# Experts: the router chain of the next block moved from its first expert step into the last step of the block before

## The chip, the cores and the metric

The kernel runs on one core of one Trainium2 chip. The metric is the device time of one execution in microseconds; before the change the median of 3 runs is 865.36 us (864.72 to 866.4).

The core's engines run their own programs side by side and meet at semaphores: PE (TensorE, matrix products; PEld is its weight load), DVE (VectorE), ACT (ScalarE), POOL (GpSimd) and SP (SyncE, which issues transfers here). Each engine works through its program in the order in which it is written.

## The reference, cut to what matters

Four sublayers, each added to x (4 x 1024 tokens, 256 features), each behind a layer normalization: an attention over 77 context tokens, a mixture of six experts, a second attention over the same context, and a feed-forward layer. The change touches the mixture of experts:

```python
z = jnp.einsum('btd,ed->bte', x, proj_w)
q = jnp.tanh(z / QUANT_TEMP)
dot = jnp.einsum('btd,ed->bte', q, anchors)
logits = -(6.0 - dot) * 0.5 / jnp.clip(routing_temp, 0.1)
topk_logits, topk_idx = jax.lax.top_k(logits, 2)
topk_w = jax.nn.softmax(topk_logits, axis=-1)
...
h = jax.nn.gelu(jnp.einsum('btd,edh->bteh', x, w1))
out = jnp.einsum('bteh,ehd,bte->btd', h, w2, expert_weights)
```

All six experts are computed for all tokens; the router gives each token two weights that aren't zero.

## The kernel before, in words

The 4096 tokens are cut into BLOCKS = 8 blocks of 512 tokens (4 tiles of 128). Each stage (attention 0, experts, attention 1, feed-forward) goes over the 8 blocks, with the work of neighbouring blocks interleaved by hand: each engine has one written-out program, and semaphores tie them together. There is no planner. The expert stage takes the time from about 250 to 443 us.

In the expert stage, g is the block and e, from 0 to 5, the expert's step. The parts, with their lines:

- `hidden(g, e)` (PE, L135): 6 matmuls of 512 columns into one of two HID banks. `gelu` (ACT, L516 and L518) reads the bank twice, into `h` (eh) and its rounded part `hh` (ehh); `rest` (DVE, L587) or `rest_pooled` (POOL, L502, experts 3 and 5) makes `hl` = h - hh (ehl).
- `output(g, e)` (PE, L629): 12 matmuls into the two OUT banks, half of them for each; each half waits until the add of the expert before has emptied its bank. PE runs `output` two steps behind `hidden`: in step e it does hidden(g, e) and then output(g, e-2), in steps 0 and 1 output(g-1, 4) and output(g-1, 5).
- `add(g, e)` (DVE, L597): 4 instructions, x += bank * weight. add(g, 0) needs the weights of the block's router.
- The router chain of a block: `project` (PE, L135 with eph and epl, 6 matmuls onto 6 rows), which waits for both halves of the block's normalized input, xh and xl; `squash` (ACT, L523, tanh); `compare` (PE, L612, 4 small fp32 matmuls into bank RD, which the profile records as 8); `router` (DVE, L555 to L567: logit, 10 comparisons, top, rank, below); `power` (POOL, L508, e to the power of below, 24 elements per partition); and `share` (DVE, L574 to L580, 4 instructions that give the weights).
- The normalization of a later block: `moments` (DVE, L90 to L98) in step 5, `invert` (POOL, L103 rstd and L105 shift), `norm` (ACT, L113, 4 instructions) in step 0 of the next block, `turn` (PE, L121, transposes) in steps 2 and 3, `lead` (ACT, L126) and `norm.rest` (DVE, L130, the low part exl) in steps 3 and 4. So norm.rest of half 1 is written in step 4, behind add(g, 2), and serves the next block.

The programs around the change, each in its order:

- PE, step 5 of block g and steps 0 and 1 of the next (L1507 to L1537): hidden(g, 5), output(g, 3), project(g+1), hidden(g+1, 0), output(g, 4), compare(g+1), hidden(g+1, 1), output(g, 5), hidden(g+1, 2), output(g+1, 0), turn, hidden(g+1, 3), output(g+1, 1), turn, hidden(g+1, 4).
- DVE (L1313 to L1334): rest(4), add(2), norm.rest, add(3), moments, rest(g+1, 0), add(4), router(g+1), rest(g+1, 1), add(5), rest(g+1, 2), share(g+1), add(g+1, 0), add(g+1, 1).
- ACT (L1131 to L1164): gelu(g, 5), squash(g+1), gelu(g+1, 0), norm, gelu(g+1, 1), gelu(g+1, 2), lead. In block 4 a weight copy (L1157) stands behind norm, in blocks 2 and 3 copies of the second attention's keys.
- POOL (L1000 to L1024): power(g), rest_pooled(3), rest_pooled(5), invert for a later block, in some blocks one more split or clear, then power(g+1).

In block 2 PE computes the keys and values of the second attention, which ACT takes from the same bank RD (`kv1_taken`).

Of the kernel before, what the change touches and what calls it, by code (L numbers as in the profile page):

```python
# [19 lines left out]
BLOCKS = B * S // N  # L20
# [786 lines left out]
def build(nc, d, out):  # L807
    m, at0, at1 = memory_map()
    place = Places(nc)
    with ExitStack() as stack:  # L810
# [12 lines left out]
        ex = Experts(nc, sem, place, norm, ps, m)  # L823
# [35 lines left out]
        with nc.Block() as block:  # L859
# [370 lines left out]
            def _(dve):  # L1230
# [82 lines left out]
                for g in range(BLOCKS):  # L1313
                    nm = LN_EXP + g + 1
                    for e in range(E):
                        if e not in ex.POOLED and (g > 0 or e > 1):
                            ex.rest(dve, g, e)
                        if e == 2:
                            ex.share(dve, g)
                        if e >= 2:  # L1320
                            ex.add(dve, g, e - 2)
                        elif g > 0:
                            ex.add(dve, g - 1, e + E - 2)
                        if e == 0 and g > 0:
                            ex.router(dve, g)
                        if e in (3, 4):
                            norm.rest(dve, nm, e - 3, ps[e - 3], ex.xh[(g + 1) % 2] if g + 1 < BLOCKS else att.xh,
                                      ex.xl[(g + 1) % 2] if g + 1 < BLOCKS else att.xl)
                        if e == 5:
                            if g + 2 >= BLOCKS:  # L1330
                                dve.wait_ge(ex.added, 2 * E * (g + 3 - BLOCKS))
                            else:
                                dve.wait_ge(att.added, 2 * (g + 3))
                            norm.moments(dve, nm + 1)  # L1334
# [59 lines left out]
                for k in range(BLOCKS * FC):  # L1394
                    g, c = divmod(k, FC)
# [24 lines left out]
            def _(pe):  # L1420
# [86 lines left out]
                for g in range(BLOCKS):  # L1507
                    nm = LN_EXP + g + 1
                    for e in range(E):
                        if g > 0 or e > 3:  # L1510
                            ex.hidden(pe, g, e)
                        if e >= 2:
                            ex.output(pe, g, e - 2)
                        elif g > 0:
                            ex.output(pe, g - 1, e + E - 2)
                        if e == 0 and g > 0:
                            if g == 3:
                                pe.wait_ge(kv1_taken, 1)
                            ex.compare(pe, g)
                        if e in (2, 3):  # L1520
                            if g == 0:
                                pe.wait_ge(att.added, 2 * (BLOCKS - 1) + e - 1)
                            else:
                                pe.wait_ge(norm.xl_ready, C * (nm - 1) + e - 1)
                            norm.turn(pe, nm, e - 2, ps[e - 2])
                        if g == 2 and e == 1:
                            pe.wait_ge(l1_in, 64)
                            pe.wait_ge(ex.logit_ready, g + 1)
                            for k in range(C):
                                nc.tensor.matmul(ex.RD[:, 64:64 + BT], wk1[:, k, :], ctx[:, k, :], start=(k == 0), stop=(k == C - 1))  # L1530
                            for b in range(B):
                                for k in range(C):
                                    last = nc.tensor.matmul(ex.RD[0:T, 384 + b * DH:384 + (b + 1) * DH], ctx[:, k, b * T:(b + 1) * T],
                                                            wv1[:, k, :], start=(k == 0), stop=(k == C - 1))
                            last.then_inc(k1_done, 1)
                    if g + 1 < BLOCKS:
                        ex.project(pe, g + 1)  # L1537
                pe.wait_ge(wl1_ready, 2)
                for c in range(C):
                    att.queries(pe, l1, BLOCKS, c)  # L1540
# [51 lines left out]
                for k in range(BLOCKS * FC):  # L1592
                    g, c = divmod(k, FC)
# [76 lines left out]
```

## Time and profile before

| what | us |
|---|---|
| median of 3 runs | 865.36 (864.72 to 866.4) |
| the profiled execution, its own time | 866.98 |
| its span in the profile | 865.2 |
| PE busy | 774.8 (90%) |
| DVE busy | 659.9 (76%) |
| ACT busy | 520.1 (60%) |
| POOL busy | 398.4 (46%) |

The profiled execution is one run; the times of rows are from it. Its own time is 1.6 us above the median. Busy shares are means over stages with different limits. A row of a timeline gives the start and length of an instruction or of a merged group, and in brackets the idle time of its engine in front of it with the instruction that ended it. The ends of PE's matmuls are modelled, and consecutive matmuls overlap in the record, so the distance between starts is what they cost.

### The profile page before, as it was taken

The numbers are of one execution on the slowest core, as the hardware profiler recorded it, in microseconds if no ns is written. First come the engines' busy times: TensorE is split into PE (matmuls) and PEld (weight loads), VectorE is DVE, ScalarE is ACT, GpSimd is POOL, SyncE is SP. The second block draws the span as 40 slices with busy tenths as digits, with TensorE's granted clock in tenths as the row PEclk, the third lists the DMA queues.
The fourth block names the chain that finished last, engine by engine and source line by source line (L and its number), as shares of the span: only waits on it lengthen the run. The fifth ranks groups of instructions, "written<-read, shape, count | busy, mean of one in ns | idle before, by whom it ended". The sixth has DMA issues, their size and how long they took to land.

```text
span 865.2 us, 13721 instructions
## 1 busy us (share of the span) xinstructions
PE 774.8 (90%) x4452; PEld 568.9 (66%) x4452; DVE 659.9 (76%) x1576; ACT 520.1 (60%) x942; POOL 398.4 (46%) x323
## 2 busy tenths in 40 slices
PE   4799999999899999999988988988879999899996
PEld 3456556666467787777754544554458888788885
DVE  7657877777768777877777888888777778787784
ACT  3455565555554455544446675666668787788774
POOL 5523322223233433443311221222159998988995
PEclk9999999999999999999988999999999999999999
DMA  6965643355200000001075446555000000000001
GB/s 216 159 164 109 146 78 72 74 107 102 70 0 1 2 3 5 2 1 50 15 97 70 59 60 110 88 75 75 3 1 1 25 1 26 25 25 2 25 25 50
DMA packets 24817, 48.01 MB, mean 55 GB/s; under 512 B 3655, under 2 KB 6856, under 8 KB 24234
## 3 DMA queue, kind: packets, MB, share of 16 engines
q1 hardware_dynamic: 23224, 46.02, 27.8%
q10 hardware_dynamic: 1522, 1.11, 0.4%
q8 instruction: 37, 0.61, 0.3%
q14 instruction: 34, 0.28, 0.1%
HBM read 11.47 MB, written 4.19 MB: 18 GB/s over the span
## 4 chain that ended last, share of the span: by engine, by line
PE 52%; DVE 18%; POOL 11%; issue 7%; ACT 5%; DMA 5%; POOLq 0%; ACTq 0%; DVEq 0%
PE bank L135 15%; PE bank L396 5%; PE bank L371 5%; PE bank L629 5%; PE bank L421 5%; DMA qst<-mt 4%; PE bank L407 4%; DVE mx L327 4%; POOL eex L508 4%; PE bank L777 4%; POOL fy L696 3%; POOL frise L689 3%; PE bank L399 2%; PE bank L121 2%; DVE x L597 2%
## 5 line engine op out<-in xcount | busy, mean ns | idle before, releaser
L301 ACT ACTIVATE pt<-bank 77x512 f32<-77x512 f32 x256 | 146.4, 589 | 123.5 <-PE bank L399 76.4
L327 DVE TENSOR_REDUCE mx<-bank 128x4 f32<-128x308 f32 x256 | 108.9, 471 | 30.3 <-PE bank L374 17.8
L396 PE MATMUL bank<-qst,l_kst 128*77 128x512 f32 (+1 forms) x256 | 106.7, 431 | 19.3 <-DMA qst<-mt 13.3
L696 POOL TENSOR_TENSOR fy<-fpart,fg 128x512 f32<-128x512 f32 x64 | 103.9, 1624 | 9.4 <-DVE fpart L737 4.8
L371 PE MATMUL bank<-l_kblk,qh 128*128 128x308 f32 x256 | 89.7, 366 | 12.0 <-DVE mx L327 9.8
L689 POOL TENSOR_TENSOR frise<-fg,fg 128x512 f32<-128x512 f32 x64 | 90.1, 1408 | 9.0 <-POOL fy L696 4.7
L103 POOL TENSOR_TENSOR rstd<-var,minus_half 128x4 f32<-128x4 f32 x32 | 33.2, 1039 | 127.6 <-DVE var L98 74.9
L396 PEld LDWEIGHTS bank<-qst,l_kst 128*77 128x77 f32 (+1 forms) x256 | 36.8, 148 | 83.2 <-issue 48.8
L277 POOL TENSOR_TENSOR ol<-ot,oh 128x512 fp32r<-128x512 f32 x32 | 43.0, 1345 | 94.2 <-ACT oh L306 62.1
L371 PEld LDWEIGHTS bank<-l_kblk,qh 128*128 128x128 f32 x256 | 49.3, 193 | 55.9 <-issue 46.8
L737 DVE SCALAR_TENSOR_TENSOR fpart<-ffixed,frise 128x512 f32<-128x512 uint16 x64 | 58.6, 915 | 33.0 <-POOL frise L689 32.8
L597 DVE SCALAR_TENSOR_TENSOR x<-bank,eweight,x 128x256 f32<-128x256 f32 x192 | 79.5, 475 | 4.4 <-PE bank L629 4.1
L777 PE MATMUL bank<-fw2h,fyh 128*128 128x256 f32 x256 | 72.3, 282 | 3.5 <-DVE fyl L743 3.5
L407 PE MATMUL bank<-pt,l_vall 128*32 128x512 f32 x512 | 69.4, 614 | 6.4 <-DVE ut L335 3.8
L113 ACT ACTIVATE xn<-x,shift,rstd 128x256 f32<-128x256 f32 x128 | 68.1, 590 | 11.6 <-POOL shift L105 11.6
L777 PE MATMUL bank<-fw2l,fyh 128*128 128x256 f32 x256 | 71.9, 281 | 0.0
L777 PE MATMUL bank<-fw2h,fyl 128*128 128x256 f32 x256 | 71.8, 281 | 0.0
L706 ACT ACTIVATE fg<-ffixed 128x512 f32<-128x512 int16 x64 | 40.4, 632 | 45.4 <-DVE ffixed L731 45.2
L629 PE MATMUL bank<-ew2h,ehh 128*128 128x256 f32 x192 | 56.6, 295 | 10.3 <-DVE x L597 10.3
L629 PE MATMUL bank<-ew2l,ehh 128*128 128x256 f32 x192 | 54.7, 285 | 0.0
L629 PE MATMUL bank<-ew2h,ehl 128*128 128x256 f32 x192 | 54.5, 284 | 0.0
L731 DVE TENSOR_SCALAR ffixed<-bank 128x512 int32<-128x512 f32 x64 | 43.7, 683 | 12.0 <-PE bank L135 11.9
(179 smaller groups left out, 2144.2 us busy)
## 6 DMA issues: line engine op xcount, KB each, us to landing
qst<-qh SPq DMA_DIRECT2D x64, 256.0 KB, 6.7
qst<-ql SPq DMA_DIRECT2D x32, 256.0 KB, 9.0
out<-x SPq DMA_DIRECT2D x8, 512.0 KB, 2.6
qst<-ml SPq DMA_DIRECT2D x8, 480.0 KB
x<-in_x SPq DMA_DIRECT2D x3, 1024.0 KB, 12.7
weights<-in_mlp_w SPq DMA_DIRECT2D x2, 1024.0 KB, 5.1
mraw<-in_mask SPq DMA_DIRECT2D x8, 154.0 KB
x<-in_x SPq DMA_DIRECT2D x2, 512.0 KB, 5.5
```

The costliest lines, as they stand in the source:

```text
L113: last = self.nc.scalar.activation(self.xn[:, t:t + 1, :], self.tile(n, t), ACT.Identity, bias=self.shift[:, t, :], scale=self.rstd[:, t, :])
L135: last = self.nc.tensor.matmul(out, w, a, start=(first and k == 0), stop=(k == len(ops) - 1))
L301: self.nc.scalar.activation(self.pt[0:T, i // 4 % 2, i % 4, :], self.bank_of(G, i)[0:T, :], ACT.Exp).then_inc(self.probs, 1)
L327: self.nc.vector.reduce_max(out, banks[u % len(banks)][:, 0:4 * T].rearrange("q (p par t) -> q p par t", p=2, par=2), AX.X).then_inc(self. ...
L371: last = self.nc.tensor.matmul(bank, self.qh[:, c, tile], keys, start=True, stop=not layer.masked)
L396: last = self.nc.tensor.matmul(out, layer.kst[rows, layer.stack(c * HC + 2 * k + par), b * T:(b + 1) * T], self.qst[rows, self.slot(G), c ...
L407: last = self.nc.tensor.matmul(self.U[32 * k:32 * k + 32, :], layer.vall[:, self.batch(G), layer.value(c * HC + 2 * k + par), :], self.pt[ ...
L597: last = self.nc.vector.scalar_tensor_tensor(tile, part, self.weight[:, g % 2, 2 * k + t, e:e + 1], tile, ALU.mult, ALU.add)
L629: last = self.nc.tensor.matmul(self.OUT[k][:, t * D:(t + 1) * D], a[:, e % self.R, tile], w[:, e, :], start=(j == 0), stop=(j == 2))
L689: self.nc.gpsimd.tensor_tensor(self.rise[:, k % 2, :], self.g1[:, k % self.R, :], self.g0[:, k % self.R, :], ALU.subtract).then_inc(self.r ...
L696: self.nc.gpsimd.tensor_tensor(self.y[:, k % 2, :], self.part[:, k % 2, :], self.g0[:, k % self.R, :], ALU.add).then_inc(self.y_ready, 1)
L777: last = nc.tensor.matmul(self.OUT[2 * (g % 2) + t // 2][:, t % 2 * D:(t % 2 + 1) * D], a[:, k % self.R, t * P:(t + 1) * P], w[:, c, :], s ...
```

## The change: what it does

The next block's projection goes from behind output(g, 3) to in front of it, inside step 5; its comparison goes from step 0 of the next block, behind output(g, 4), to step 5 behind output(g, 3); the router on DVE goes from step 0 of the next block, behind add(g, 4), to step 5 behind add(g, 3) and in front of the moments. The wait for `kv1_taken` goes along with the comparison. The programs of ACT, POOL and SP are unchanged.

```diff
@@ DVE
                         elif g > 0:
                             ex.add(dve, g - 1, e + E - 2)
-                        if e == 0 and g > 0:
-                            ex.router(dve, g)
                         if e in (3, 4):
                             norm.rest(dve, nm, e - 3, ps[e - 3], ex.xh[(g + 1) % 2] if g + 1 < BLOCKS else att.xh,
                                       ex.xl[(g + 1) % 2] if g + 1 < BLOCKS else att.xl)
+                        if e == 5 and g + 1 < BLOCKS:
+                            ex.router(dve, g + 1)
                         if e == 5:
...
@@ PE
                         if g > 0 or e > 3:
                             ex.hidden(pe, g, e)
+                        if e == 5 and g + 1 < BLOCKS:
+                            ex.project(pe, g + 1)
                         if e >= 2:
                             ex.output(pe, g, e - 2)
                         elif g > 0:
                             ex.output(pe, g - 1, e + E - 2)
-                        if e == 0 and g > 0:
-                            if g == 3:
+                        if e == 5 and g + 1 < BLOCKS:
+                            if g == 2:
                                 pe.wait_ge(kv1_taken, 1)
-                            ex.compare(pe, g)
+                            ex.compare(pe, g + 1)
...
-                    if g + 1 < BLOCKS:
-                        ex.project(pe, g + 1)
                 pe.wait_ge(wl1_ready, 2)
```

## Rows read from the trace of the kernel before

**Rows 1.** Busy time by window, from output(g,1) to output(g+1,1); window, its length, engines.

```profile
core 0: us, PE busy (x) PEld busy (x) DVE busy (x) ACT busy (x) POOL busy (x), PEclk, DMA share, GB/s
...
284.47:307.84 23.37, 22.99 (x150) 19.56 (x151) 17.65 (x60) 9.60 (x18) 9.29 (x8) 1.00 0.01 1
...
330.36:352.34 21.98, 21.07 (x130) 17.63 (x131) 17.74 (x60) 11.85 (x23) 7.85 (x5) 1.00 0.00 1
...
374.87:397.38 22.51, 21.01 (x130) 17.61 (x131) 17.74 (x60) 11.33 (x21) 9.90 (x7) 1.00 0.14 48
```

**Rows 2.** The chain of waits, block 6; start, length, what.

```profile
390.76 4.71 POOL eex L508
```

**Rows 3.** Timeline of PE, blocks 6 and 7; start, length, line, tiles, idle before.

```profile
392.38 0.36 PE L629 MATMUL bank<-ew2h,ehh 128*128 128x256 f32 x1
...
395.48 0.40 PE L135 MATMUL bank<-exl,ew1h 128*128 128x512 f32 x1
397.38 0.35 PE L629 MATMUL bank<-ew2h,ehh 128*128 128x256 f32 x1 [1.51 <-DVE x L597]
...
399.25 0.48 PE L135 MATMUL bank<-exh,ew1h 128*128 128x512 f32 x1
...
403.67 0.36 PE L629 MATMUL bank<-ew2h,ehh 128*128 128x256 f32 x1
...
405.17 0.39 PE L135 MATMUL bank<-exh,eph 128*6 128x512 f32 x1
...
406.56 0.39 PE L135 MATMUL bank<-exh,ew1h 128*128 128x512 f32 x1
...
409.46 1.05 PE L612 MATMUL bank<-eanchors,eq 6*128 6x6 f32 x8
```

**Rows 4.** Timeline of ACT, the same stretch.

```profile
406.76 0.59 ACT L523 ACTIVATE eq<-bank 6x512 f32<-6x512 f32 x1 [1.93 <-PE bank L135]
...
410.11 2.08 ACT L113 ACTIVATE xn<-x,shift,rstd 128x256 f32<-128x256 f32 x4 [0.88 <-POOL shift L105]
```

**Rows 5.** Timeline of DVE, the same stretch.

```profile
393.57 0.69 DVE L587 TENSOR_TENSOR ehl<-eh,ehh 128x512 fp32r<-128x512 f32 x1 [0.55 <-ACT ehh L518]
...
398.37 1.66 DVE L597 SCALAR_TENSOR_TENSOR x<-bank,eweight,x 128x256 f32<-128x256 f32 x4 [0.34 <-PE bank L629]
...
402.04 0.69 DVE L587 TENSOR_TENSOR ehl<-eh,ehh 128x512 fp32r<-128x512 f32 x1 [1.42 <-ACT ehh L518]
...
404.22 0.68 DVE L130 TENSOR_TENSOR exl<-bank,exh 128x512 fp32r<-128x512 f32 x1
404.82 1.65 DVE L597 SCALAR_TENSOR_TENSOR x<-bank,eweight,x 128x256 f32<-128x256 f32 x4
406.39 1.39 DVE L90 BATCH_NORM_STATS2 stats<-x 128x6 f32<-128x256 f32 x4
...
411.44 0.23 DVE L555 TENSOR_SCALAR elogit<-bank,ehalf 128x24 f32<-128x24 f32 x1
...
412.96 0.17 DVE L567 TENSOR_TENSOR ebelow<-elogit,etop 128x24 f32<-128x24 f32 x1
...
413.87 1.65 DVE L597 SCALAR_TENSOR_TENSOR x<-bank,eweight,x 128x256 f32<-128x256 f32 x4
```

**Rows 6.** Timeline of POOL, the same stretch.

```profile
408.60 1.01 POOL L103 TENSOR_TENSOR rstd<-var,minus_half 128x4 f32<-128x4 f32 x1 [2.35 <-issue]
...
413.28 4.69 POOL L508 TENSOR_TENSOR eex<-eeuler,ebelow 128x24 f32<-128x24 f32 x1 [3.26 <-DVE ebelow L567]
```

**Rows 7.** Timeline of ACT, block 4, behind norm.

```profile
345.08 0.62 ACT L1157 ACTIVATE l_wqh<-weights 128x512 fp32r<-128x512 f32 x1
```

**Rows 8.** The chain of waits, block 2, keys of the second attention.

```profile
300.63 1.04 PE bank L1530 x4
```

**Rows 9.** Busy time by window, end of the first attention; columns as in rows 1.

```profile
228.00:232.00 4.00, 2.67 (x15) 0.95 (x14) 3.97 (x3) 3.33 (x7) 3.43 (x2) 1.00 0.00 0
232.00:236.00 4.00, 2.65 (x14) 2.60 (x15) 1.47 (x5) 0.00 (x0) 1.20 (x1) 0.79 0.57 163
236.00:240.00 4.00, 4.00 (x24) 2.70 (x23) 1.69 (x3) 0.59 (x1) 0.00 (x0) 0.79 0.04 9
```

## The prediction

> **What bounds the kernel now.** I read the windows first, one for each block of the expert stage, cut where output(g,1) starts. Seven such blocks lie between 262 and 420 us; they take 22.5 us each, with two exceptions [rows 1]: 23.4 us where the keys and values of layer 1 are put in, 22.0 us in the block whose power was shortest. TensorE is busy for 21.0 of 22.5 us at the full granted clock. The chain of waits runs through the power in every block but that of the keys [rows 2]: it takes 4.7 us on GpSimd and is what the change wants to start sooner. In TensorE's timeline [rows 3] the price of that chain shows as one pause per block: the last matmul of hidden(6,3) starts at 395.48 and output(6,1) could follow 0.23 us later, at 395.71, but starts at 397.38. So 1.67 us a block is what a perfect cure of the power chain could give, 12 us over seven blocks.
>
> The next question is which chain comes second. The other engines' timelines [rows 4, 5, 6] show a ring that is nearly as long as the one through the power, and I check it link by link, since the change puts its work into this ring. hidden(6,4) at 399.25 [rows 3] gives rest(4) at 402.04; add(2) and the second exl follow back to back, then add(3) at 404.82 and the moments at 406.39 [rows 5]; rstd at 408.60 [rows 6]; the norm at 410.11, which waited for shift [rows 4]; behind it on the same queue stands the gelu of expert 1, and behind that gelu, on DVE, rest(1) and add(5) at 413.87 [rows 5]. output(7,0) waits for half of add(5): one block earlier (22.51 us) that is 391.36 to 392.38 [rows 3], 1.02 us. From there TensorE needs 397.38 - 392.38 - 1.67 = 3.33 us to output(1) and 399.25 - 397.38 = 1.87 us to hidden(4). The ring is 413.87 + 1.02 + 3.33 + 1.87 - 399.25 = 20.84 us: **the spare of this ring is 22.51 - 20.84 = 1.67 us**, and no more.
>
> **The change, part by part.** No instruction is added or removed. The projection (6 matmuls, 406.56 - 405.17 = 1.39 us [rows 3]), the comparison (4 small matmuls in 8 records, 1.05 us [rows 3]) and the router's 14 DVE instructions (411.44 to 412.96 and 0.20 for the last, 1.72 us [rows 5]) move. The ACT and POOL programs stay. No DMA is issued or moved, and nothing is moved past SP's queue.
>
> 1. *Project before output(3).* Project waits for both halves of exl of the next block. The second is written from 404.22 for 0.68 us [rows 5], so it is there at 404.90; with 0.15 us for the signal (an estimate: 1.02 us less the 0.87 that half an add takes) project starts at 405.05. Today that is hidden, for project starts at 405.17. In its new place TensorE is free for it at about 403.67, where output(3) starts now [rows 3]. **TensorE waits 1.4 us in front of project**, and output(3) is queued behind: it starts at 405.05 + 1.39 = 406.44, 2.77 us later than now.
>
> 2. *add(3)* waits for half of output(3). After a waiting output that was 398.37 - 397.38 = 0.99 us [rows 3, 5], so add(3) starts at 407.43, not 404.82: 2.61 us later (DVE idles meanwhile). It takes 406.39 - 404.82 = 1.57 us, to 409.00.
>
> 3. *Comparison.* Squash starts 0.2 us after project's end now (406.76 [rows 4]), so about 406.65, and takes 0.6 us; output(3) lasts to 407.94, so the comparison does not wait. It ends at 407.94 + 1.05 = 408.99 and the router starts at about 409.05, with nothing lost.
>
> 4. *Router before the moments.* The moments start at 409.05 + 1.72 = 410.77, where they now start at 406.39: **4.4 us late, against a spare of 1.67.** 2.6 us are from project's wait, 1.7 us from the router.
>
> 5. *The rest of the ring.* Moments to rstd 2.21, to the norm 1.51, norm to add(5) 3.76, add(5) to output(0) 1.02 us [rows 3 to 6]: output(7,0) at 419.27 where it now is at 414.89. Then 3.33 + 1.87 us to hidden(7,4) at 424.47. **The block is 25.2 us, 2.7 more than 22.5.**
>
> 6. *The power.* In POOL's program invert stands in front of the next power. Today the power starts 3.26 us after POOL is free [rows 6]; with the change ebelow is there before var, but the power waits behind rstd and shift and starts at about 414.5, later on the clock than the 413.28 of now. It ends at 419.2. DVE is at add(5) until 419.9 and rest(2) until 420.5, so share no longer waits for it; output(7,1) can follow 0.86 (share) + 1.02 us later, at 422.4, and TensorE is there at 419.27 + 3.33 = 422.6. The old pause is gone, as wanted. Two others stand in its place, since DVE reaches add(4) only after router, moments and rest(0), at about 413.4: output(6,5) waits 1.2 us, output(7,0) 1.9 us. The first is covered by the second.
>
> *The blocks that differ.* The block with the 4.17 us power takes 21.98 us now [rows 1]; with the ring as bound that advantage is lost: 0.5 us more. In the same block ACT copies a weight between norm and gelu (0.5 us [rows 7]), now in the ring: 0.5 more. The keys' 2.1 us of matmuls (half of them in [rows 8]) go in front of hidden(2) and are covered by output(0)'s new wait; that block comes out at about 26.0 against 23.37, 0.1 less than the rule. GpSimd's extra splits in two blocks delay the power by 1.3 us, up to where share is anyway. **Sum: 7 x 2.7 + 0.5 + 0.5 - 0.1 = 19.8 us.** The last block has no next router and its tail is unchanged. The profiled execution took 866.98 us (span 865.2) and would become 886.8; the median of the runs is 1.6 us less, 865.36, so I say 885.
>
> *Bounds.* Where I took 0.99 us from output to add, a running output might give 0.9; the signal to project is between 0.05 and 0.3 us; the router's 1.72 may be 1.6. Together 0.3 us a block either way, 2 us in all. The ring's links were seen only with their present neighbours; I allow the same again.
>
> *A rule against the trace.* GpSimd's power is beside DVE work with two SBUF inputs today: rest(2), 393.57, falls into the power of 390.76 to 395.46 and takes 0.69 us, as the one at 402.04 with POOL idle does [rows 2, 5]. The two don't hold each other up here. The Trainium skill ("SBUF — State Buffer", section "SBUF: two separate sides") says the opposite: such a DVE instruction and a GpSimd instruction share a port pair that is locked for the whole instruction, and the other "fully blocks". By it rest(1), ready at 417.6, would wait for the power's end at 419.2, and each block would be 1.6 us longer.
>
> **The rivals.** (A) *Ends faster:* the ring through moments and norm has room that the rows don't show, and only the power chain counts. Place: the norm on ACT. It decides if output(0) would still be there within 22.5 us, so if the moments can be 4.4 us late at no cost. Then the 1.67 us pause goes and the 1.4 us in front of project come, with 0.2 us of small waits gone: -0.5 a block, 862; if in addition project didn't wait, up to 7 x 1.67 = 11.7 us less, 854. Against it: ACT waited for shift in each of the blocks (0.88 us [rows 4]). (B) *Only one delay bites,* the router's 1.7 us or project's 2.6 being hidden: +0.1 to +1.0 us a block, 866 to 872. Against it: both are in front of the moments in one queue. (C) *The clock.* In 228:236 TensorE was busy 5.3 of 8 us, and the granted clock of the 8 us from 232 was 0.79 [rows 9]: of the levels 2.4 and 1.2 GHz the lower one for 8 x 2 x 0.21 = 3.4 us. The new block has 1.2 and 1.9 us of waiting with 2.9 of work between, so 2.9 of 6. If the clock falls there, in TensorE's part of the ring, 3.4 us at half speed cost 1.7 us a block: 897. Against it: after the pause of 1.51 us in front of 397.38 the matmuls keep their pace. (D) *The port lock* above, as a mechanism of this kernel: rest(1) behind the power, +1.6 us a block, 896. Its page is the one named there. (E) *Nothing to see:* the waits only change places.
>
> **How the numbers follow.** Forecast 0.75; A 0.06; B 0.07, of it 0.01 within 0.2%; C 0.09; D 0.02; E 0.01. A measurement of this kernel tells about 0.2%, 1.7 us, from no change. Faster 0.06, same 0.02, slower 0.92. The forecast's own range is 881 to 889. For 8 in 10 I widen it to 875 at the bottom (a part of B) and 893 at the top (a clock that falls in some blocks, C).
>
> **What would show it.** Right: TensorE's idle time in front of project, released by exl, of 1.2 to 1.4 us and seven times; no wait of eexs for the power; the moments some 4.4 us later after output(3)'s old place; waits of output(0) of 1.7 us or more for add(5); ACT's wait for shift in front of the norm longer than 0.88; blocks of 25.2 us. Wrong: blocks of 21 to 22 us, which would mean that the moments had room; project starting straight behind hidden(5), which would break step 1; a power that starts before rstd, which would break step 6; a granted clock under 1.00 in this stage, which would be C.

## The result, and the profile after

| | before | after |
|---|---|---|
| median of 4 runs each, us | 865.04 (864.41 to 866.4) | 889.78 (888.8 to 893.36) |
| ratio | 1 | 1.029 (95%: 1.027 to 1.031) |
| span of the profiled run, us | 865.2 | 887.5 |
| PE busy in it, us | 774.8 | 776.8 |

The change costs 24.7 us; the prediction's sum was 19.8. The measured 889.78 us lies in the wide range of 875 to 893, but above the 881 to 889 that the prediction gave to its forecast itself. In a second measurement it took 888.25 against 865.73 us.

The windows first, as in [rows 1], but cut where the moments of a block start, the event that the prediction turned on. The column PEclk, third from the end, is the granted clock. The two windows that are left out are the block of the keys (301.15 to 326.85, 25.70 us at a clock of 1.00) and the last one.

```profile
core 0: us, PE busy (x) PEld busy (x) DVE busy (x) ACT busy (x) POOL busy (x), PEclk, DMA share, GB/s
274.51:301.15 26.64, 22.58 (x132) 19.00 (x131) 17.65 (x60) 10.13 (x20) 8.26 (x5) 0.94 0.00 1
326.85:351.92 25.07, 21.01 (x133) 17.55 (x132) 17.67 (x61) 13.48 (x28) 9.14 (x6) 1.00 0.02 5
351.92:379.06 27.14, 22.56 (x132) 18.87 (x131) 17.65 (x60) 11.16 (x22) 8.28 (x5) 0.94 0.01 2
379.06:404.14 25.08, 20.99 (x132) 17.54 (x131) 17.66 (x60) 11.13 (x22) 9.56 (x6) 1.00 0.00 1
404.14:430.77 26.63, 22.57 (x133) 19.01 (x131) 17.66 (x61) 10.14 (x20) 9.57 (x6) 0.94 0.12 41
```

Two kinds of block stand there: 25.1 us at a clock of 1.00, and 26.6 us at 0.94 (27.1 in block 4, where the weight copy is). The forecast was 25.2, and 25.7 for block 4. In the long ones TensorE is busy 1.6 us longer with as many instructions. Cut finer, one of them shows where:

```profile
404.14:412.75 8.61, 5.81 (x36) 4.66 (x35) 5.79 (x21) 5.06 (x10) 6.15 (x4) 1.00 0.27 85
412.75:414.00 1.25, 1.25 (x8) 1.25 (x9) 1.25 (x4) 0.00 (x0) 0.83 (x1) 0.78 0.68 275
414.00:417.00 3.00, 3.00 (x14) 2.77 (x13) 2.28 (x8) 0.60 (x1) 0.00 (x0) 0.52 0.00 0
417.00:430.77 13.77, 12.52 (x79) 10.33 (x77) 8.33 (x30) 4.48 (x9) 2.59 (x2) 1.00 0.01 1
```

Behind the wait for output(0), which ends at 412.75, the clock is at its lower level for some 3 us. In windows of 1 us the same shows from 284 to 287, 362 to 366 and 441 to 444: in four of seven blocks.

The timelines of PE, DVE, POOL and ACT around block 7, to be read against [rows 3 to 6]:

```profile
419.45 0.48 PE L135 MATMUL bank<-exh,ew1h 128*128 128x512 f32 x1
425.16 0.40 PE L135 MATMUL bank<-exh,eph 128*6 128x512 f32 x1 [1.25 <-DVE exl L130]
426.55 0.28 PE L629 MATMUL bank<-ew2h,ehh 128*128 128x256 f32 x1
428.06 1.05 PE L612 MATMUL bank<-eanchors,eq 6*128 6x6 f32 x8
434.39 0.36 PE L629 MATMUL bank<-ew2h,ehh 128*128 128x256 f32 x1 [0.87 <-DVE x L597]
439.38 0.36 PE L629 MATMUL bank<-ew2h,ehh 128*128 128x256 f32 x1 [1.94 <-DVE x L597]
```

```profile
424.42 0.68 DVE L130 TENSOR_TENSOR exl<-bank,exh 128x512 fp32r<-128x512 f32 x1
427.45 1.66 DVE L597 SCALAR_TENSOR_TENSOR x<-bank,eweight,x 128x256 f32<-128x256 f32 x4 [2.35 <-PE bank L629]
429.15 0.24 DVE L555 TENSOR_SCALAR elogit<-bank,ehalf 128x24 f32<-128x24 f32 x1
430.77 1.40 DVE L90 BATCH_NORM_STATS2 stats<-x 128x6 f32<-128x256 f32 x4
432.77 0.69 DVE L587 TENSOR_TENSOR ehl<-eh,ehh 128x512 fp32r<-128x512 f32 x1
437.76 0.69 DVE L587 TENSOR_TENSOR ehl<-eh,ehh 128x512 fp32r<-128x512 f32 x1 [2.74 <-ACT ehh L518]
438.37 1.65 DVE L597 SCALAR_TENSOR_TENSOR x<-bank,eweight,x 128x256 f32<-128x256 f32 x4
```

```profile
432.99 1.32 POOL L103 TENSOR_TENSOR rstd<-var,minus_half 128x4 f32<-128x4 f32 x1 [6.54 <-issue]
434.67 4.16 POOL L508 TENSOR_TENSOR eex<-eeuler,ebelow 128x24 f32<-128x24 f32 x1
```

```profile
434.69 2.08 ACT L113 ACTIVATE xn<-x,shift,rstd 128x256 f32<-128x256 f32 x4 [2.87 <-POOL shift L105]
```

Project waits for exl; output(3) stands behind it; add(3) idles DVE for 2.35 us; the router takes its turn, and only then come the moments. GpSimd idled for 6.5 us up to rstd, although the router's result was there 2.1 us earlier, at 430.9: rstd is in front of the power in its program. output(5), at 434.39, and output(0), at 439.38, wait for their adds.

### The profile page after: what moved, and what is told of

It is laid out like the page before. It is cut to its first block, busy times and chain, and to the rows that moved or that the text cites. A ratio compares the mean times of both kernels' runs of the same rounds, so it can differ in the third digit from the quotient of the medians.

```text
span 887.5 us, 13721 instructions
## 1 busy us (share of the span) xinstructions
PE 776.8 (88%) x4452; PEld 572.2 (64%) x4452; DVE 660.5 (74%) x1576; ACT 518.4 (58%) x942; POOL 396.4 (45%) x323
## 3 DMA queue, kind: packets, MB, share of 16 engines
q1 hardware_dynamic: 23224, 46.02, 27.1%
## 4 chain that ended last, share of the span: by engine, by line
PE 51%; DVE 19%; issue 12%; ACT 7%; POOL 7%; DMA 4%; DVEq 0%; POOLq 0%; ACTq 0%
PE bank L135 14%; PE bank L371 5%; PE bank L396 5%; PE bank L777 5%; PE bank L421 5%; DMA qst<-mt 4%; PE bank L629 4%; PE bank L407 4%; DVE mx L327 4%; PE bank L121 2%; POOL fy L696 2%; PE bank L399 2%; DVE x L597 2%; POOL frise L689 2%; ACT xn L113 2%
## 5 line engine op out<-in xcount | busy, mean ns | idle before, releaser
L103 POOL TENSOR_TENSOR rstd<-var,minus_half 128x4 f32<-128x4 f32 x32 | 35.2, 1101 | 154.2 <-issue 79.2
L113 ACT ACTIVATE xn<-x,shift,rstd 128x256 f32<-128x256 f32 x128 | 68.1, 590 | 25.6 <-POOL shift L105 25.6
L516 ACT ACTIVATE eh<-bank 128x512 f32<-128x512 f32 x48 | 28.4, 591 | 49.7 <-PE bank L135 48.7
L502 POOL TENSOR_TENSOR ehl<-eh,ehh 128x512 fp32r<-128x512 f32 x16 | 20.7, 1293 | 81.4 <-ACT ehh L518 81.4
L629 PEld LDWEIGHTS bank<-ew2h,ehh 128*128 128x128 f32 x192 | 37.4, 195 | 28.8 <-DVE ehl L587 14.6
```

What stands on the lines that cost most here:

```text
L113: last = self.nc.scalar.activation(self.xn[:, t:t + 1, :], self.tile(n, t), ACT.Identity, bias=self.shift[:, t, :], scale=self.rstd[:, t, :])
L629: last = self.nc.tensor.matmul(self.OUT[k][:, t * D:(t + 1) * D], a[:, e % self.R, tile], w[:, e, :], start=(j == 0), stop=(j == 2))
```

## The experiments

**The projection alone** (timed with the next three against the same runs of before, 865.58 us):

```diff
                             ex.hidden(pe, g, e)
+                        if e == 5 and g + 1 < BLOCKS:
+                            ex.project(pe, g + 1)
...
-                    if g + 1 < BLOCKS:
-                        ex.project(pe, g + 1)
```

> Only the projection is moved in front of output(g, 3); comparison and router stay where they were before. Ring theory (project's wait for exl delays output(3), add(3) and the moments by 2.6 us; DVE then reaches rest(0), add(4) and the old router 1.8 us later than before, so the power chain binds again): TensorE waits 1.2 to 1.4 us in front of project in seven blocks, blocks of 24.3 us, about 878 us. Rival (project's wait costs nothing by itself, only the router in front of the moments does): 865 to 867 us.

875.68 us, ratio 1.012 (1.010 to 1.015). In the trace project waits in seven blocks, 8.8 us in all (1.25 each), the clock stays at 1.00 in this stage, and blocks take 23.6 to 24.2 us (24.6 where the keys are). Most of what the clean blocks (23.55 us) have under the 24.3 expected is the power, which took 4.16 us here, not 4.70; share still waited 0.35 us for it. The two blocks of 24.2 us are those in which a split on GpSimd held the router's comparisons (1.44 and 1.54 us in place of 0.93), which the run with the splits moved takes up. The rival is out: project's wait has a price of its own.

**The router alone**, in front of the moments, with the projection where it was (cut, against the kernel before):

```diff
+                        if e == 0 and g > 0:
+                            if g == 3:
+                                pe.wait_ge(kv1_taken, 1)
+                            ex.compare(pe, g)
                         if e >= 2:
                             ex.output(pe, g, e - 2)
...
+                        if e == 5 and g + 1 < BLOCKS:
+                            ex.router(dve, g + 1)
                         if e == 5:
```

> The projection stays behind output(g, 3) as before; the comparison goes one output earlier (behind hidden(g+1, 0)), and the router stands in front of the moments as in the changed kernel. Ring theory: the comparison ends at the same time as in the changed kernel, so the moments start 4.4 us late as there and blocks are 25 us or more although TensorE never waits for exl: 885 to 890 us. Rival (the 1.2 us wait in front of project is what costs, the router's 1.7 us on DVE is hidden): 866 to 872 us.

894.44 us, ratio 1.034 (1.031 to 1.037). TensorE never waited for exl, and still its blocks take what they take in the changed kernel:

```profile
275.00:300.25 25.25, 22.57 (x131) 18.91 (x130) 17.66 (x61) 10.26 (x19) 8.26 (x5) 0.93 0.00 1
378.62:405.43 26.81, 22.61 (x131) 18.93 (x130) 17.56 (x61) 11.12 (x21) 9.58 (x6) 0.94 0.00 1
```

The moments' start is what counts, by whichever way it is delayed. The clock fell in each of the six blocks that aren't that of the keys, behind waits of 2.27 us in front of output(5) and up to 1.94 (2.46 in block 4) in front of output(0), without any wait of project. In the first block of the fence it fell behind the wait for output(5), and the shorter wait that was left in front of output(0) took the loss in, as in two more; in the second it cost 1.6 us, as in two more. With that this stage is as long as in the changed kernel with its four falls (178.1 us from the first moments to the last, against 178.7). The profiled run, 891.87 us, took 2.6 us more than that of the changed kernel, and these lie behind the stage, where the clock also fell, in other places.

**The moments in front of the router**, all else as in the changed kernel:

```diff
-                        if e == 5 and g + 1 < BLOCKS:
-                            ex.router(dve, g + 1)
...
                             norm.moments(dve, nm + 1)
+                        if e == 5 and g + 1 < BLOCKS:
+                            ex.router(dve, g + 1)
```

> The changed kernel with one swap: on DVE the moments stand in front of the next block's router. Ring theory: the moments are 2.6 us late, not 4.4, the power starts at the same time as GpSimd's invert ends, blocks of 23.5 us, wait for output(0) under 0.5 us and a full clock: about 873 us. Rival (the power chain or the projection's place decides, the order of moments and router doesn't): 885 to 890 us.

876.36 us, ratio 1.014 (1.010 to 1.018). The clean block is as expected:

```profile
272.84:296.24 23.40, 21.25 (x131) 17.47 (x130) 17.66 (x60) 10.26 (x19) 8.27 (x5) 1.00 0.00 1
```

So the order of two neighbours on DVE is worth 1.7 us a block, the router's length. What lies above the expected 873 us shows in the stage of the profiled run (itself the slowest of the four, 881.05 us) as two things: one fall of the clock, and in two blocks a rest(0) of 1.80 us in place of 0.69, which the last section takes up.

**TensorE's waits filled** with matmuls whose results nobody reads:

```diff
+                        if (e == 1 and g > 0) or (e == 2 and g > 0):
+                            for k in range(4 if e == 1 else 6):
+                                nc.tensor.matmul(ex.RZ[:, :], ex.w1h[:, 0, 0:DE], ex.xh[g % 2][:, 0, :], start=True, stop=True)
                         if e >= 2:
                             ex.output(pe, g, e - 2)
```

> The changed kernel, and TensorE does 4 idle matmuls of 512 columns in front of output(g, 5) and 6 in front of output(g+1, 0), into the bank of the projection, where it waited anyway; their results are used nowhere. Clock theory (the 5 us above the forecast come from the granted clock that falls to 0.5 behind the waits of output(5) and output(0)): the clock stays at 1.00, all blocks take 25.1 us, 885 us. Rival (the 5 us are longer links of the ring, the clock follows and costs nothing): 889 to 891 us.

884.79 us (884.3 to 886.42), ratio 1.023 (1.021 to 1.025), with ten matmuls more in each block:

```profile
275.16:300.20 25.04, 23.21 (x142) 19.41 (x141) 17.65 (x60) 10.14 (x20) 8.27 (x5) 1.00 0.00 1
351.70:377.31 25.61, 23.25 (x143) 19.45 (x142) 17.65 (x61) 11.17 (x22) 8.28 (x5) 1.00 0.01 2
402.37:427.45 25.08, 23.24 (x142) 19.43 (x141) 17.66 (x61) 10.14 (x20) 9.57 (x6) 1.00 0.13 43
```

The clock stays at 1.00 to the end of the stage, no block but that of the keys is over 25.6 us, and block 4 has the 0.5 us of its weight copy. The block of the keys took 26.42 us, 0.7 more than in the changed kernel: there the ten matmuls don't all fit into waits. This settles the missing 5 us: they are the clock. It also measures the forecast without it: 885 us, 0.7 of them the fill's own.

**exl earlier**, in the changed kernel, into time in which DVE idled (a second set; before took 865.83 us in its runs):

```diff
+                        if e == 4:
+                            norm.rest(dve, nm, e - 3, ps[e - 3], ex.xh[(g + 1) % 2] if g + 1 < BLOCKS else att.xh,
...
                         if e not in ex.POOLED and (g > 0 or e > 1):
                             ex.rest(dve, g, e)
...
-                        if e in (3, 4):
+                        if e == 3:
```

> The changed kernel, and on DVE the second half of exl is written in front of rest(g, 4) instead of behind add(g, 2), into time in which DVE idled. Ring theory: TensorE no longer waits in front of project, output(3) is 1.5 us late instead of 2.8, the moments 2.9 us instead of 4.4, blocks of 23.7 us: about 875 us. Rival (project's wait is covered by the later wait for add(5), the ring is set by the router's place): 885 us or more.

873.42 us, ratio 1.009 (1.007 to 1.012). No wait in front of project is left, and blocks take 23.65 us (24.2 that of the keys and block 4). The waits of output(5) and output(0) are still 0.87 and 1.94 us, as in the changed kernel, but the clock did not fall in the stage in the one execution that was traced.

**Router behind the moments, projection unmoved.** From the ring follows a version that should gain: the comparison one output earlier, which nothing waits for, and the router directly behind the moments.

```diff
-                        if e == 0 and g > 0:
-                            ex.router(dve, g)
...
                             norm.moments(dve, nm + 1)
+                        if e == 5 and g + 1 < BLOCKS:
+                            ex.router(dve, g + 1)
...
+                        if e == 0 and g > 0:
...
+                            ex.compare(pe, g)
                         if e >= 2:
                             ex.output(pe, g, e - 2)
```

> The kernel before with the comparison one output earlier (behind hidden(g+1, 0)) and the router directly behind the moments, in front of rest(g+1, 0); the projection stays. Ring theory: the moments keep their time, the power starts at 410.9 instead of 413.3 of the old clock, share waits for rest(2) instead of the power: blocks of 21.7 us instead of 22.5, about 860 us. Rival (the router costs the ring wherever it stands in front of rest(0)): 865 us or more.

865.1 us, ratio 0.999 (0.997 to 1.0005): no difference that the runs tell. The clean blocks are as worked out, but not all are clean:

```profile
270.28:291.97 21.69, 21.04 (x132) 17.48 (x131) 17.66 (x61) 10.39 (x19) 8.30 (x5) 1.00 0.00 1
359.86:382.66 22.80, 21.04 (x132) 17.47 (x131) 18.67 (x60) 11.37 (x21) 9.62 (x6) 1.00 0.00 1
```

DVE is busy 1.0 us longer in the second with as many instructions. There are three clean blocks; two take 22.8 us, more than before the change.

**share in front of rest(2)**, in addition:

```diff
+                        if e == 2:
+                            ex.share(dve, g)
                         if e not in ex.POOLED and (g > 0 or e > 1):
                             ex.rest(dve, g, e)
-                        if e == 2:
-                            ex.share(dve, g)
```

> As the run with the router behind the moments, and share in front of rest(g, 2) on DVE. Ring theory: output(1) waits for nothing, TensorE sets the block with a wait of 0.6 us in front of output(5): blocks of 21.3 us, about 857 us. Rival (rest(2) was covered): as that run, 860 us.

861.42 us (857.09 to 866.2), ratio 0.995 (0.992 to 0.998). Clean blocks take 21.1 us, the two long ones 22.2, one 21.7 and that of the keys 23.3. The times of this kernel spread by 9 us, and the spread goes with the granted clock of the whole execution: the three at a mean of 0.988 took 857.1 to 858.2 us, the four at 0.974 to 0.976 took 864.3 to 866.2.

**exl earlier on top of that:**

> As the run with share first, and the second half of exl in front of rest(g, 4). Ring theory: add(3) is no longer held by exl, 0.1 to 0.2 us a block less: about 856 us. Rival: no difference to the run before it.

864.49 us, ratio 0.998 (0.995 to 1.000). Its clean blocks are 21.1 us too: TensorE sets them, and exl has nothing to give. From the first moments to the last it took 152.7 us, against 152.6 without this step. In the profiled run the clock fell behind the first block's wait for output(1). The expected gain is not there, and the 3 us between the medians aren't in these blocks.

**GpSimd's splits behind the power.** In the long blocks the router's comparisons took 2.04 us in place of 0.93, just while GpSimd split a weight. This is the second measurement of the run with share first, DVE and then POOL:

```profile
362.38 0.24 DVE L555 TENSOR_SCALAR elogit<-bank,ehalf 128x24 f32<-128x24 f32 x1 [0.68 <-PE bank L612]
362.65 2.04 DVE L561 TENSOR_TENSOR eabove<-elogit 128x20 f32<-128x20 f32 x10
```

```profile
362.91 0.22 POOL L105 TENSOR_TENSOR shift<-minus_mean,rstd 128x4 f32<-128x4 f32 x1
363.21 1.35 POOL L1019 TENSOR_TENSOR l_wql<-weights,l_wqh 128x512 fp32r<-128x512 f32 x1
```

```diff
                     ex.power(pool, g)
+                    if g == 3:
+                        pool.wait_ge(kt1_ready, 2)
+                        nc.gpsimd.tensor_tensor(l1.kl[:], ...
...
+                    if g == 5:
+                        pool.wait_ge(wh1_ready, 1)
+                        nc.gpsimd.tensor_tensor(l1.wql[:], ...
...
+                    if g == 6:
+                        pool.wait_ge(wh1_ready, 2)
+                        nc.gpsimd.tensor_tensor(l1.wol[:], ...
...
-                    if g == 2:
...
-                    if g == 4:
...
-                    if g == 5:
```

> As the run with share first, and GpSimd's three splits (keys, query and output weights of the second attention) stand behind the next power instead of in front of it. If DVE's comparisons of the router (two SBUF inputs) are held while such a split runs (0.93 became 2.04 us in two blocks and 1.61 in one), all ten comparisons take 0.93 us in every block, the three long blocks lose 0.7, 1.1 and 1.1 us, and the time is about 3 us under that of the run with share first. Rival (the long comparisons have another cause, or the splits hold other DVE work in their new place): no difference.

859.6 us (856.07 to 862.8), ratio 0.993 (0.991 to 0.995), the fastest. The comparisons take 0.93 us in every block, and every block but that of the keys takes 21.1 to 21.2 us:

```profile
357.12:378.28 21.16, 20.89 (x132) 17.48 (x131) 18.21 (x60) 11.38 (x21) 9.59 (x6) 1.00 0.00 1
378.28:399.43 21.15, 20.88 (x132) 17.46 (x131) 18.20 (x60) 10.39 (x19) 9.59 (x6) 1.00 0.15 51
```

The expected 3 us are in the trace: from the first moments to the last 149.8 us, against 152.6. The medians differ by 1.4 us with ranges that overlap, so by time alone it is not told from the kernel that it grew from, which was run again beside it:

> The run with share first once more, beside the run with the splits moved: 861 us; and under the kernel before by 4 us.

861.02 us, ratio 0.996 (0.994 to 0.998), as the first time. With them ran the changed kernel:

> The changed kernel beside the others on one chip: 889 us, with a granted clock of 0.5 for about 3 us in some of the seven blocks, always behind the wait for output(0); the blocks without it take 25.1 us, as all blocks did where TensorE's waits were filled.

888.25 us (887.56 to 893.86), with five falls of the clock in the stage.

## Why the prediction was right, step by step

- *Step 1, project's wait.* 1.25 us shown in each of seven blocks (1.4 with the overlap of the records), as forecast.
- *Steps 2 and 3.* add(3) came 0.90 us behind output(3), where I had 0.99; DVE idled 2.35 us; the comparison waited for nothing.
- *Step 4, the delay of the moments against the spare.* From hidden(4) to the moments it was 7.14 us before [rows 3, 5] and is 430.77 - 419.45 = 11.32: 4.2 us late where 4.4 were forecast. Both parts were tested apart. The spare of 1.67 says that a clean block takes 20.84 us plus the delay of the moments: with the router behind them (2.45 us late) 23.3, measured 23.4; with exl early (2.74 late) 23.6, measured 23.65; with the router alone in front of them (4.36 late) 25.2, measured 25.2; in the changed kernel (4.18 late) 25.0, measured 25.1.
- *Step 5, the ring.* From hidden(6,4) to output(7,0) 439.38 - 419.45 = 19.93 us; forecast 20.02. The clean block is 25.1 against 25.2. The wait of output(5) is 0.87 us where 1.2 were forecast, that of output(0) 1.94 against 1.9.
- *Step 6, the power.* It started behind rstd and shift, 0.02 us in front of the norm. It was not sooner, as forecast: 15.22 us behind hidden(4), against 14.03 before. Share did not wait for it.
- *The blocks that differ.* Block 4: 25.6 us at full clock, forecast 25.7. Block of the keys: 25.7, forecast 26.0.
- *The sum* lacked a term. What failed is the weighing of rival (C): I gave 0.09 to a clock that falls and left it out of the forecast. It fell in four blocks and cost 1.5 to 1.6 us each (26.63 - 25.08 = 1.55). With the corrected links the sum is 19.8 - 6 x 0.1 - 0.3 + 4 x 1.5 = 24.9. In the traces the stage is 25.0 us longer, from project(0) to the moments of the last block (204.1 against 179.1). The medians differ by 24.7, the two profiled executions by 22.3, since that of before lay 1.9 us above its median. The price of 1.7 us a block was near; it did not come in every block. The forecast's own range was missed by 0.8 us, and the time is inside the wide range because its top was set for a clock that falls in some blocks: the ring was forecast, the number of falls was not.
- *Rival (D)* did not occur: rest(1) took 0.69 us beside the power, at 437.76. But the sentence that the two engines don't hold each other up was wrong, as the last section shows. The ring's link from rstd to norm became 1.70 us where I had 1.51: rstd took 1.32 us in place of 1.01, and shift 0.20 in place of 0.32. The power, with no rest beside its start, took 4.16 us in place of 4.70, and nothing waited for it.
- *Rivals (A), (B), (E)* are out by the runs above: the blocks fit a room of 1.67 us for the moments to within 0.1.

## What to carry to other kernels

Before moving a chain forward, find the second longest ring and its spare, link by link, and ask in which queues the moved step now stands in front of that ring's work: here 4.2 us went in front of the moments, against a spare of 1.67, to start a power that GpSimd's own order did not let start (no run changes that order in the changed kernel). The same idea gains 0.4 to 0.7% when the moved steps stand behind the ring's work and share in front of rest(2); without the second it gained nothing that the runs tell. And where new waits of TensorE follow each other closely, price the clock as a term of the sum, not only as a rival.

## What the runs showed of the hardware

**The clock and its surroundings.** Six blocks of the changed kernel have two waits of 0.87 and at least 1.94 us, with 3 us of work between (the block of the keys has no long second one). The same two waits left the clock at 1.00 in all six when project did not wait (exl earlier), and let it fall in four of six, and in five of six on the second measurement, when project's wait of 1.25 us stood some 9 us ahead of them. Filled with matmuls they never let it fall. Before the change one wait of 1.5 us a block did nothing.

But project's wait is not needed for a fall: with the router alone there was none, output(5) waited 2.27 us, and the clock fell in six of six blocks, in three behind that wait and in three behind output(0)'s of 1.94 us or more. And one wait can do: behind the single wait of 2.1 us in front of output(1) of the first block it fell in three of the four traced executions of the last kernels (exl on top, splits moved, share first the second time) and not in the fourth (share first the first time), which is the same program as the third. So more or longer waits close together go with more falls, the same waits don't always give the same answer, and where a fall comes in one execution can't be told from the waits alone. Each kernel was traced once or twice; how the chip weighs the waits these runs don't show.

**DVE and GpSimd hold each other up, by who starts first.** rest (DVE, two SBUF inputs of 512 columns, 0.69 us) and GpSimd's instructions, in all kernels of this study:

| GpSimd's instruction | what DVE does as it starts | its time, us |
|---|---|---|
| power | nothing with two large SBUF inputs, or a rest starts 0.36 us later or more | 4.16 |
| power | a rest that started 0.32 us before | 4.39 |
| power | a rest that started 0.23 us before | 4.48 |
| power | a rest that started 0.01 us before | 4.70 |
| rstd | idle, or a rest starts 0.66 us later | 1.01 |
| rstd | a rest that started 0.22 us before | 1.32 |

GpSimd's time grows by what is left of the rest, less about 0.14 us: with 0.68, 0.46 and 0.37 us left of a rest of 0.69 the power is longer by 0.54, 0.32 and 0.23. The other way round, a split on GpSimd (512 columns, 1.3 us) held a rest that started 0.03 us behind it to 1.80 us, and the router's ten comparisons to 2.04. The rest of 1.80 us is in the run with the moments in front of the router, DVE and POOL:

```profile
372.34 1.80 DVE L587 TENSOR_TENSOR ehl<-eh,ehh 128x512 fp32r<-128x512 f32 x1
372.31 1.28 POOL L1019 TENSOR_TENSOR l_wql<-weights,l_wqh 128x512 fp32r<-128x512 f32 x1
```

Two starts only 0.03 us apart don't settle who goes first. In the same run the smaller split of the keys started 0.03 us in front of a rest, and here it was the split that was held (1.42 us; 0.86 in the changed kernel):

```profile
325.42 0.69 DVE L587 TENSOR_TENSOR ehl<-eh,ehh 128x512 fp32r<-128x512 f32 x1
325.39 1.42 POOL L1015 TENSOR_TENSOR l_kl<-l_kt,l_kh 128x308 fp32r<-128x308 f32 x1
```

The power, once started, held no rest (0.69 us, from 0.36 to 3.9 us into it). It has only 24 elements per partition to read, against the split's 512; whether that is the reason no run tests. That the 4.17 us power of [rows 1]'s short block was short fits the table: its rest(1) came 0.43 us later, behind the weight copy. The Trainium skill ("SBUF — State Buffer", section "SBUF: two separate sides") has this as an exclusive lock of a shared port pair, taken by whichever starts first, for the whole instruction. The trace agrees in both directions for the splits' long reads; for the power, "for the whole instruction" does not hold on DVE's side.
